# The copy of the values out of PSUM made in two halves, each half of the score products waiting for its own

## What is computed

```python
def _mhsa(x, Wq, Wk, Wv, Wr):          # x: 2048 x 39 x 64, dh = 32
    q, k, v = (x @ Wq), (x @ Wk), (x @ Wv)      # each reshaped to (B, n, HEADS, dh)
    scores = jnp.einsum('bihd,bjhd->bhij', q, k)
    attn = jax.nn.softmax(scores, axis=-1)
    out = jnp.einsum('bhij,bjhd->bihd', attn, v).reshape(B, n, D)
    return jax.nn.relu(out + x @ Wr)

att = embed_x = emb_table[X + offsets[None, :]]
for i in range(3):
    att = _mhsa(att, WQ[i], WK[i], WV[i], WR[i])
att_output = relu(att.reshape(B, FLAT) @ Wlin)
h = relu(embed_x.reshape(B, FLAT) @ W1 + b1)
h = relu(h @ W2 + b2)
y = sigmoid(att_output + relu(h @ W3 + b3))
```

## Time and profile before

| | |
|---|---|
| median of 3 runs | 2033.41 us (2029.62 to 2035.76) |
| profiled execution, span | 2034.7 us |
| busy: PE, PEld | 94%, 83% |
| busy: DVE, ACT, POOL | 83%, 66%, 44% |
| instructions | 105018 |

### The profile page before, as it was taken

One profiled execution on the slowest core, in us unless ns is written; L12 is line 12 of the kernel. 1 busy time (PEld: TensorE's weight loads), 2 busy tenths in 40 slices (PEclk: granted clock), 3 DMA queues, 4 the chain that ended last, 5 costly groups with the idle time before them and its releaser, 6 DMA issues.

```text
span 2034.7 us, 105018 instructions
## 1 busy us (share of the span) xinstructions
PE 1914.9 (94%) x44960; PEld 1692.9 (83%) x44960; DVE 1690.5 (83%) x3771; ACT 1351.5 (66%) x3609; POOL 893.3 (44%) x949
## 2 busy tenths in 40 slices
PE   1499999999999999999999999999999999999998
PEld 0387888888888888888888888888888888888887
DVE  3477889889898888979888898888889898888987
ACT  1366666667666676766766776666776667676665
POOL 6544354444535454354544435354453545444000
PEclk9899999999999999999999999999999999999998
DMA  4210111111111111111111111111111111110000
GB/s 113 60 31 25 31 27 32 29 30 31 28 33 28 31 30 29 32 28 32 29 30 30 29 33 27 32 28 30 31 28 34 28 32 29 30 31 26 20 20 16
DMA packets 67859, 64.71 MB, mean 32 GB/s; under 512 B 24056, under 2 KB 54792, under 8 KB 67400
## 3 DMA queue, kind: packets, MB, share of 16 engines
q1 hardware_dynamic: 47432, 37.52, 6.3%
q0 software_dynamic: 19968, 20.49, 5.3%
HBM read 27.24 MB, written 0.01 MB: 13 GB/s over the span
## 4 chain that ended last, share of the span: by engine, by line
PE 86%; DVE 5%; issue 4%; ACT 3%; another core or an unknown queue 1%; POOL 1%; SPq 0%; DMA 0%; ACTq 0%
PE SV L479 20%; PE Ob L496 14%; PE X L464 12%; PE X L457 8%; PE X L459 5%; PE X L458 5%; PE Mb L432 3%; PE Mb L433 3%; PE Mb L434 3%; PE Ob L457 3%; PE Ob L458 2%; PE Ob L459 2%; PE Ob L423 2%; PE Mb L450 1%
## 5 line engine op out<-in xcount | busy, mean ns | idle before, releaser
L355 POOL DMA_INDIRECT emb<-L_rec_emb_table,idx_t x624 | 646.9, 1037 | 752.4 <-PE Ob L496 551.2
L742 DVE TENSOR_REDUCE den<-sd 103x16 f32<-103x624 f32 x384 | 308.0, 802 | 225.6 <-ACT sd L616 211.0
L479 PE MATMUL SV<-yv,xs 64*39 64x142 f32 x12288 | 456.0, 285 | 21.2 <-ACT v_sb L618 13.4
L479 PEld LDWEIGHTS SV<-yv,xs 64*39 64x39 f32 x12288 | 349.8, 113 | 68.0 <-issue 39.6
L600 ACT ACTIVATE xs<-Ob 128x312 f32<-128x312 f32 x256 | 110.4, 431 | 383.6 <-PE Ob L496 383.6
L722 DVE TENSOR_REDUCE mx<-SV 103x8 f32<-103x312 f32 x768 | 332.7, 473 | 37.0 <-PE SV L479 28.7
L496 PEld LDWEIGHTS Ob<-pt,v_sb 39*32 39x32 f32 x12288 | 272.1, 106 | 96.5 <-issue 96.0
L464 PE MATMUL X<-ident,pn 103*103 103x103 f32 x3072 | 343.0, 255 | 0.0
L496 PE MATMUL Ob<-pt,v_sb 39*32 39x39 f32 x12288 | 326.4, 198 | 8.9 <-issue 8.5
L332 POOL COPY xs<-embT 64x256 f32<-64x256 f32 x300 | 239.1, 797 | 211.6 <-ACT embT L560 80.7
L727 DVE TENSOR_TENSOR sd<-SV,mx 103x312 f32<-103x312 f32 x768 | 330.2, 470 | 0.1
(11 more groups left out here) (81 smaller groups left out, 2749.2 us busy)
## 6 DMA issues: line engine op xcount, KB each, us to landing
v_x<-v_sb SPq DMA_DIRECT2D x768, 39.0 KB
emb<-L_rec_emb_table,idx_t POOLq DMA_INDIRECT x624
xs<-L_rec_W SPq DMA_DIRECT2D x19, 256.0 KB
w<-L_rec_W SPq DMA_DIRECT2D x1, 512.0 KB
idx_in<-r_X SPq DMA_DIRECT2D x1, 312.0 KB, 3.8
b_b<-L_rec_b SPq DMA_DIRECT2D x1, 256.0 KB
b_b<-L_rec_b SPq DMA_DIRECT2D x1, 128.0 KB
w_b<-L_rec_W SPq DMA_DIRECT2D x1, 128.0 KB
```

The source lines that it names most:

```text
L355: nc.gpsimd.indirect_dma_start(out=emb[:, n % ER, f % 2 * D:(f % 2 + 1) * D], out_offset=None, in_=table, in_offset=bass.IndirectOffsetOnA ...
L479: last = nc.tensor.matmul(SV[64 * b:64 * b + F, at:at + YR], x_pair(u, e, p), yv[64 * e:64 * e + D, l, p, :], start=True, stop=True, skip_ ...
L742: nc.vector.tensor_reduce(den[:], pe_sb[:], AX.X, ALU.add).then_inc(den_ready, 1)
```

## The change

The copy at L618 becomes two, one for each half of SV's banks, and each adds one to `v_ready`. The eight score products of half `j` wait for half `j` of the copy. SP's DMAs of `v_x` wait for both halves.

```diff
@@ SyncE
             for u in range(TOTAL):
-                sp.wait_ge(v_ready, u + 1)
+                sp.wait_ge(v_ready, 2 * (u + 1))
@@ TensorE, scores(u)
                 for j in range(2):
-                    if j == 0:
-                        at_least(pe, v_ready, u)
+                    at_least(pe, v_ready, 2 * (u - 1) + j + 1)
                     for pp in range(2):
@@ ScalarE
                     at_least(act, o_ps, u - VS + 1)
-                    nc.scalar.copy(v_sb[:, u % VS, :, :, :], sv_values).then_inc(v_ready, 1)
+                    for j in range(2):
+                        nc.scalar.copy(v_sb[:, u % VS, :, regions(j), :], sv_values[:, :, regions(j), :]).then_inc(v_ready, 1)
```

## The result

The changed kernel takes 2018.8 us (median of 4 runs, 2015.4 to 2024.5) against 2033.8 for the kernel before (median of 4). The ratio is 0.9925, 95% interval 0.9908 to 0.9943: 15 us less. The forecast was 2020.7.

The account below looks back on a forecast made before the run. TensorE's own queue was taken as the bound. A span of 2034.7 us, less 20.2 of holds, plus 7.5 coming back, gave 2022.0; with the span 1.3 above the median, the forecast was 2020.7, range 2011 to 2034.

Parts of the forecast that it names:

- The reading of the holds: Before the scores, TensorE waits for the L618 copy in 182 of 380 steps, 20.2 us in all.
- the row of 13.4 us: List of waits: TensorE waiting for the L618 copy in 7 places, 12.3 us of it once; called misleading.
- The half copy: On ACT at L618, 256 columns take about 0.38 us, so the first half is there 0.21 us earlier.
- The second wait: Between the 16th and 17th score matmul records: never ends last, 0.2 us to spare; taken as zero, at most 0.08 a step.
- Nearly all of the 20.2 us goes: Before the scores: single holds are mostly 0.21 us or less, so the earlier first half removes nearly all.
- it gets its work earlier: DVE, idle 225.6 us ahead of L742, gets work earlier when ACT and TensorE are earlier; no separate size given.
- what comes back: At TensorE's L496 weight loads, part of the saved time returns as issue waits: 6.4 to 11 us, taken as 7.5.
- The row of unheld steps: Scores to next step's first product: 1.89 us in one unheld step, 1.83 in another and in a held one.
- Rival 1: Everything comes back as issue time, TensorE's sequencer being the true bound: 2031 to 2034 us; chance 0.15.
- Rival 2: ACT operations have a high fixed cost, so the first half gains only 0.09 us per hold: 2026 us; chance 0.06.
- Rival 3: The wait inside the score products stops loads running ahead, 0.08 us in each of 384 steps: 2052 us; chance 0.08.
- Rival 4: Nothing comes back, as the sequencer catches up elsewhere: 2013 us; chance 0.11.

Follow-up runs that it names:

- e3: The kernel before with an idle 128-column copy on ACT ahead of the copy of the values: 2084.9 us, ratio 1.0245.
- e1: The changed kernel with the copy still split, but the first score product waiting for both halves: 2042.2 us, ratio 1.0038 to the kernel before.
- e2: The kernel before with its wait for the whole copy also ahead of the ninth score product: 2034.8 us, ratio 1.0009.
- e7: The changed kernel unaltered, run again in a series at the 1989 us level: 1959.7 us, ratio 0.9858 to the kernel before.
- e5: The changed kernel with both copy halves moved ahead of the exp on ACT: 2007.3 us, ratio 1.0093 to the kernel before of its series.
- e10: The kernel before with DVE's dense output apart, product in step 10 and sum in step 12: 1988.7 us, ratio 0.9992.
- e11: The kernel before unaltered, run again in a later series: 2034.5 us.

## Why the prediction was right, and where not

*The reading of the holds held.* 0.82 us between transposes and scores is the unheld distance, 0.15 us the distance from copy to scores, and what was over it was time: 16 us of holds fewer in two series, 50 more in e3; in e1, with 18 more, other parts took half of it back. The chain by line and the row of 13.4 us would have hidden this. The idle time of the loads shows a part of it, as the prediction said: without the long wait at the start and 0.10 a step it was 17.0 us and is 52.4 - 9.6 - 38.4 = 4.4 now, a fall of 12.6 where the starts give 16.0.

*The half copy was priced right:* 388 ns against 0.38 us, and two take 0.67 together against 0.64. The Trainium skill, ScalarE: Activation LUTs, Rules for kernel authors, gives about 0.3 us and 0.83 ns an element for an ACTIVATE with its bias as a pointer operand, a condition that the prediction left out and that this plain copy does not meet. By that budget one half would take 0.51 and two 1.02; here queued copies overlap and the measured 0.67 decides.

*The second wait* was rightly costed at nothing. e2 shows a met one to be free, and in the changed trace the first product of the second half never starts less than 0.35 us after its copy ended, against 0.14 where a wait decides.

*Two terms were wrong and cancelled in part.* "Nearly all of the 20.2 us goes" was too much: 5.0 stayed, since in steps 4 to 8 of a tile DVE is late, the exp with it, and then even the first half. The prediction said of DVE that it gets its work earlier and left it there; the 0.79 us of dense output in step 2 shows on no row that it cites. And "what comes back", 7.5 us at L496, did not come there: the idle time ahead of those loads is 96.5 and 96.1, and the small gaps between the attended products fell from 7.4 to 5.9 us. The row of unheld steps (1.89 against 1.83) had been read as a cause. But from scores to the next step 49 of 197 unheld steps took 1.83 in the kernel before, and 221 of 333 do in the changed one. Instead 5.1 us came back ahead of the residual product, a place which the prediction did not name. 3.4 of them are in the steps (19 to 23 and 0 to 2 of a tile) in which the residual product waits for DVE's L698, and the rest mostly in a few single steps elsewhere. The sum, 16.0 - 5.1 + 2.1 - 0.4, is 12.6 us against 12.7 forecast, and that closeness is luck: two errors of 4.2 and 2.4 us stood against each other, and the scores gave 2.1 that no term had. The medians are 15.0 apart, with an interval of 11.6 to 18.7, so they do not tell these sums apart.

*Rival 1* (all of it comes back as issue time) falls by e3 and by the row of L495. *Rival 2* falls by the 388 ns. *Rival 3* falls by e2. *Rival 4* (nothing comes back, 20 us gained) is nearest to the 29 us of e7, but there too the holds gave only 16.5, and the rest has other places.

## What to carry to other kernels

Where an in-order queue waits for the end of a copy out of PSUM, it is worth trying to let the first consumer wait for the first part only. The split paid here because two short copies overlap (0.67 us together against 0.59 for one), and it cost 8 us where the waits were not split with it (e1). Look for such holds in the distance between the starts of neighbouring matmuls and in the idle time of the weight loads, not in the idle time of matmuls, which overlap and hide them. And measure the slack on both sides of the point: after this change 0.19 us more on ACT costs 20 us instead of 51, and 0.5 us more ahead of the exp costs more than the whole gain (e5).

## What was not expected of the hardware

The same kernel ran at 2034 and at 1989 us, on one and the same chip in two series (e10's series and e11's). By the traces, the start of the program is 18 to 21 us shorter at the lower level (77.9 us to step 3 in e10, 95.9 in e11 and 99.1 at first), and the long pauses inside the attended products 20 to 25 us shorter (11.7 against 32.0 and 36.6); the rest of the step is alike within 3 us in each part.

More than half of the difference at the start is one wait. In each of the eight traces of the higher level the score loads of step 1 wait for 9.6 to 12.8 us, and in none of the six of the lower level. With TensorE idle in this wait its granted clock falls to the lower of its two levels (1.2 of 2.4 GHz), and stays at 1.00 where the wait is missing, as the stretch from 60 to 100 us shows, in the kernel before and in e10 (the last three numbers are the granted clock as a share, the share of the DMA engines and GB/s):

```profile
60.00:100.00 40.00, 19.72 (x214) 14.95 (x215) 17.10 (x37) 12.17 (x31) 19.42 (x21) 0.83 0.10 21
60.00:100.00 40.00, 37.18 (x682) 31.46 (x683) 29.01 (x66) 24.23 (x69) 25.19 (x25) 1.00 0.15 33
```

So the levels can be told apart within the first 100 us. What makes ACT late in that step, for which the scores wait (12.3 us of the 13.4 in the earlier trace rows), is open.

The pauses stand in step 9 of most tiles, with TensorE's loads waiting for nothing but "issue". They are 1.35 us long in the kernel before at the higher level and 0.53 in e10 at the lower; the program changes them too, to 1.52 in the changed kernel and 0.9 in e1. What sets the level, and the pause, stays open.
